# The last path's three products merged into two in the second FFN product: 14 matmuls a tile instead of 15

## The reference, cut to what matters

```python
x = x + xattn(layernorm(x), ctx, mask, Wq, bq, Wk, bk, Wv, bv, Wo, bo)
h = layernorm(x)
x_mixed = k0 * h[s-1] + k1 * h[s] + k2 * h[s+1]
hp = einsum('bsd,pdm->bspm', x_mixed, W1) + b1           # P = 9 paths, m = 64
stacked_paths = einsum('bspm,pmd->bspd', hp, W2) + b2    # d = 256
scores = tanh(x_mixed @ Wo1 + bo1) @ Wo2 + bo2
weights = one_hot(argmax(scores), 9)
collapsed = einsum('bspd,bsp->bsd', stacked_paths, weights)
x = x + layernorm(h + collapsed) * gamma + beta
```

## Time and profile before

| what | value |
|---|---|
| median of 3 runs | 330.58 us (330.08 to 331.59) |
| the profiled execution, its own time | 329.75 us |
| its span, first to last instruction | 328.0 us |
| PE, PEld busy | 303.1 us (92%), 228.2 us (70%) |
| DVE, ACT, POOL busy | 264.7, 181.9, 218.0 us |
| mean granted TensorE clock | 0.994 |

### The profile page before, as it was taken

One profiled execution on the slowest core, in us unless ns is written; L12 is line 12 of the kernel. 1 busy time (PEld: TensorE's weight loads), 2 busy tenths in 40 slices (PEclk: granted clock), 3 DMA queues, 4 the chain that ended last, 5 costly groups with the idle time before them and its releaser, 6 DMA issues. The chain is left out here.

```text
span 328.0 us, 7236 instructions
## 1 busy us (share of the span) xinstructions
PE 303.1 (92%) x2799; PEld 228.2 (70%) x2803; DVE 264.7 (81%) x612; ACT 181.9 (55%) x282; POOL 218.0 (66%) x259
## 2 busy tenths in 40 slices
PE   3889998899989999999999999999999999999991
PEld 2564564566669766896779767886779667967990
DVE  2876799998499796999699796989498878695876
ACT  1455724725963677358853778267552855266520
POOL 0391145872495499957986499957886598539454
PEclk9999999999999999999999999999999999999997
DMA  7942020020020010300120010000100010001003
GB/s 212 242 106 81 2 82 1 2 81 2 1 74 9 0 44 21 82 1 3 66 81 1 2 64 4 2 0 2 66 0 3 1 66 2 0 2 64 3 0 128
DMA packets 20587, 13.16 MB, mean 40 GB/s; under 512 B 10113, under 2 KB 20426, under 8 KB 20554
## 3 DMA queue, kind: packets, MB, share of 16 engines
q1 hardware_dynamic: 18914, 12.14, 12.8%
q10 hardware_dynamic: 1640, 0.57, 0.8%
HBM read 8.51 MB, written 4.19 MB: 39 GB/s over the span
## 5 line engine op out<-in xcount | busy, mean ns | idle before, releaser
L1536 POOL TENSOR_TENSOR rs<-ve,halfneg 128x4 f32<-128x4 f32 x22 | 23.7, 1075 | 37.0 <-DVE ve L1180 37.0
L1630 POOL TENSOR_TENSOR hml<-hs,hmh 128x512 fp32r<-128x512 f32 x28 | 35.1, 1282 | 4.3 <-ACT hmh L985 4.3
L1217 DVE TENSOR_REDUCE mx<-ps 128x16 f32<-128x1024 f32 x32 | 37.6, 1216 | 0.3 <-PE ps L553 0.3
L922 ACT ACTIVATE e<-ps 128x1024 f32<-128x1024 f32 x32 | 31.1, 1023 | 9.5 <-PE ps L592 9.2
L719 PE MATMUL ps<-w2h,hmh 128*128 128x256 f32 (+1 forms) x140 | 35.1, 288 | 0.0
L720 PE MATMUL ps<-w2l,hmh 128*128 128x256 f32 (+1 forms) x140 | 34.1, 280 | 0.0
L1337 DVE TENSOR_TENSOR hs<-hs,ps 128x512 f32<-128x512 f32 x28 | 18.5, 683 | 17.3 <-PE ps L699 17.3
L630 PE MATMUL ps<-wo,osb 128*128 128x256 f32 x128 | 31.4, 390 | 0.2 <-DVE osb L1244 0.2
L1595 POOL TENSOR_TENSOR y<-xh2f,gms 128x256 f32<-128x256 f32 x24 | 20.4, 880 | 16.2 <-DVE xh2f L1189 16.2
L1561 POOL TENSOR_TENSOR x<-xin,bos 128x256 f32<-128x256 f32 x32 | 22.8, 744 | 10.2 <-DVE rDs L1235 9.6
L975 ACT ACTIVATE hs<-ps,b1s 128x512 f32<-128x512 f32 x28 | 19.0, 687 | 16.1 <-PE ps L456 16.1
(11 more groups left out here) (176 smaller groups left out, 804.5 us busy)
## 6 DMA issues: line engine op xcount, KB each, us to landing
xin<-in_x SPq DMA_DIRECT2D x8, 512.0 KB, 3.7
out<-y SPq DMA_DIRECT2D x6, 512.0 KB, 2.9
min_<-in_mask_Bx1xSxS_ik SPq DMA_DIRECT2D x8, 128.0 KB, 3.7
hs<-in_L_ffn_W SPq DMA_DIRECT2D x2, 288.0 KB
hs<-in_L_ffn_W SPq DMA_DIRECT2D x1, 512.0 KB
out<-y SPq DMA_DIRECT2D x2, 256.0 KB, 2.1
out<-xin SPq DMA_DIRECT2D x2, 256.0 KB, 2.3
cst<-in_constants SPq DMA_DIRECT2D x1, 384.0 KB, 6.7
```

The source lines that it names most:

```text
L922: nc.scalar.activation(e[:, 4 * half + g:4 * half + g + 3:2, :], ps[:, 2 + 2 * g:4 + 2 * g, :], ACT.Exp).then_inc(s_e, 1)
L1217: v.tensor_reduce(mx[:, k, :].rearrange("p (a h) -> p a h", a=2), ps[:, bank:bank + 2, :].rearrange("p a (h s) -> p a h s", s=SK), AX.X, A ...
L1536: g.tensor_tensor(ln[7][:, :], ln[6][:, :], halfneg[:, :], ALU.pow).then_inc(s_r, 1)
L1630: g.tensor_tensor(L.lo(m, r), L.selected(m, r), L.hi(m, r).bitcast(F32), ALU.subtract).then_inc(L.s_hl, 1)
```

## The change

Block 4 had 55 unused rows. The change puts path 8's rounded rows a second time into rows 64 to 127 of the remainder's buffer, and W2[8] a second time into rows 64 to 127 of w2h. The matmul lo x w2h of block 4 then gives lo x w2h and hi x w2h of path 8 at once, and the matmul hi x w2h of block 4 is left out. b2 can then no longer come from w2h; its rounded part and its remainder lie instead in rows 64 to 72 and 73 to 81 of w2l, and the one-hot is written twice (columns 0 to 8 and 9 to 17 of the 64 that `rep` passes), so that hi x w2l adds both.

```diff
         def rows_of(m):
-            return P if m < 4 else DM + NPATH
+            return P if m < 4 else DM + 2 * NPATH
+        def lo_rows_of(m):
+            return P if m < 4 else DM
...
+            def hi_below(self):
+                return hml[DM:, NM - 1, :]
...
+            def hi_below(self):
+                return xTl[DM:, 0, :]
...
                 load(w2_32[0:DM, 4, :], W2[8], s_wf)
-                load(w2_32[DM:DM + NPATH, 4, :], b2, s_wf)
+                load(w2_32[DM:, 4, :], W2[8], s_wf)
+                for i in range(2):
+                    load(y[DM + i * NPATH:DM + (i + 1) * NPATH, 1, :], b2, s_wf)
...
             def w2_product(b, j, k, terms, L=usual):
-                        nc.tensor.matmul(o, L.hi(m, r)[:, ks], w2h[0:r, m, :], start=(m == 0), stop=False)
+                        if m < 4:
+                            nc.tensor.matmul(o, L.hi(m, r)[:, ks], w2h[:, m, :], start=(m == 0), stop=False)
                         nc.tensor.matmul(o, L.hi(m, r)[:, ks], w2l[0:r, m, :], start=False, stop=False)
...
                             pe.wait_ge(L.s_hl, L.first + L.count(b, j, NM, m + 1))
-                        mm = nc.tensor.matmul(o, L.lo(m, r)[:, ks], w2h[0:r, m, :], start=False, stop=(m == NM - 1))
+                            if m == NM - 1:
+                                pe.wait_ge(L.s_hb, L.count(b, j, 1, 1))
+                        mm = nc.tensor.matmul(o, L.lo(m, P)[:, ks], w2h[:, m, :], start=False, stop=(m == NM - 1))
...
             def selected_hi(b, j, m, L=usual):
                 nc.scalar.activation(L.hi(m, r), L.selected(m, r), ACT.Copy).then_inc(L.s_hh, 1)
+                if m == NM - 1:
+                    nc.scalar.activation(L.hi_below(), L.selected(m, DM), ACT.Copy).then_inc(L.s_hb, 1)
...
             def ffn_weights_lo():
-                v.tensor_tensor(w2l[0:r, 4, :], w2_32[0:r, 4, :], w2h[0:r, 4, :].bitcast(F32),
-                                ALU.subtract).then_inc(s_w2l, 1)
+                v.tensor_tensor(w2l[0:DM, 4, :], w2_32[0:DM, 4, :], w2h[0:DM, 4, :].bitcast(F32), ALU.subtract)
+                b2_parts = w2l[DM:DM + 2 * NPATH, 4, :]
+                v.tensor_copy(b2_parts, b2_32).then_inc(s_b2h, 1)
+                dve.wait_ge(s_b2h, 1)
+                v.scalar_tensor_tensor(out=b2_parts, in0=b2_parts.bitcast(F32), scalar=cst[DM:DM + 2 * NPATH, C_LB:C_LB + 1],
+                                       in1=b2_32, op0=ALU.mult, op1=ALU.add).then_inc(s_w2l, 1)
...
             def argmax(b, j, L=usual):
-                v.tensor_tensor(oh[:, :, 0:NPATH], iota, per_tile(gidx), ALU.is_equal).then_inc(s_oh, 1)
+                twice = [P, NT, 2, NPATH]
+                v.tensor_tensor(oh[:, :, 0:2 * NPATH].rearrange("p k (a n) -> p k a n", a=2),
+                                cst[:, C_IO:C_IO + NPATH].rearrange("p (k a n) -> p k a n", k=1, a=1).broadcast_to(twice),
+                                gidx[:, :].rearrange("p (k a n) -> p k a n", a=1, n=1).broadcast_to(twice),
+                                ALU.is_equal).then_inc(s_oh, 1)
```

More of the change, by code:

```diff
@@ L58 @@
 C_LO = C_IO + NPATH
-C_CST = C_LO + 1
+C_LB = C_LO + 1
+C_CST = C_LB + 1
 C_BC = C_CST
@@ L92, in constants @@
     c[:, C_LO:C_LO + 1] = np.where(r % 32 < 16, 0, -1)
+    c[:, C_LB:C_LB + 1] = np.where(r < DM + NPATH, 0, -1)
     c[:, C_IO:C_IO + NPATH] = np.arange(NPATH) - NPATH
@@ L190, in layer_program @@
         bc32 = y[:, 0, :].rearrange("p (c n) -> p c n", c=KD)
+        b2_32 = y[DM:DM + 2 * NPATH, 1, :]
         ps = stack.enter_context(nc.psum_tensor("ps", [P, 8, CH], F32))
@@ L247, in layer_program @@
         s_lf, s_lfa, s_lfv = sem("last_ffn_filled"), sem("last_ffn_read_by_act"), sem("last_ffn_read_by_dve")
+        s_hb, s_lhb, s_b2h = sem("last_path_hi_below_lo"), sem("last_chunk_last_path_hi_below_lo"), sem("b2_hi")
         s_lhh, s_lhl, s_lones = sem("last_selected_hi"), sem("last_selected_lo"), sem("last_b2_selector_ones")
@@ L285, in layer_program, with __init__ @@
         class Path:
-            def __init__(self, filled, read_by_act, read_by_dve, hi_done, lo_done):
+            def __init__(self, filled, read_by_act, read_by_dve, hi_done, lo_done, hi_below):
                 self.s_f, self.s_fa, self.s_fv, self.s_hh, self.s_hl = filled, read_by_act, read_by_dve, hi_done, lo_done
+                self.s_hb = hi_below
             def filled(self, b, j, use):
@@ L364, in x @@
                 return ps[:, self.banks[("w2a", "w2b", "w2c")[group]], i * D:(i + 1) * D]
-        usual, last = Usual(s_f, s_fa, s_fv, s_hh, s_hl), Last(s_lf, s_lfa, s_lfv, s_lhh, s_lhl)
-        behind = BehindSteps(s_f, s_fa, s_fv, s_hh, s_hl)
+        usual, last = Usual(s_f, s_fa, s_fv, s_hh, s_hl, s_hb), Last(s_lf, s_lfa, s_lfv, s_lhh, s_lhl, s_lhb)
+        behind = BehindSteps(s_f, s_fa, s_fv, s_hh, s_hl, s_hb)
         last_y = xin[:, 1]
         def rows_of(m):
-            return P if m < 4 else DM + NPATH
+            return P if m < 4 else DM + 2 * NPATH
+        def lo_rows_of(m):
+            return P if m < 4 else DM
         block = stack.enter_context(nc.Block())
@@ L700, in rep @@
                         else:
-                            mm = nc.tensor.matmul(o[DM:, ks], oh[:, k, :], ident_b,
-                                                  start=True, stop=True)
+                            mm = nc.tensor.matmul(o[DM:, ks], oh[:, k, :], ident_b, start=True, stop=True)
                 mm.then_inc(L.s_f, 1)
@@ L881, in split_ffn_weights @@
                 nc.scalar.activation(w2h[:, 0:4, :], w2_32[:, 0:4, :], ACT.Copy)
-                r = DM + NPATH
-                nc.scalar.activation(w2h[0:r, 4, :], w2_32[0:r, 4, :], ACT.Copy).then_inc(s_w2h, 1)
+                nc.scalar.activation(w2h[:, 4, :], w2_32[:, 4, :], ACT.Copy).then_inc(s_w2h, 1)
             def mask_copy(b, j, mask_bank):
@@ L1340, in last_selected_lo @@
             def last_selected_lo(b, j, m):
-                r = rows_of(m)
+                r = lo_rows_of(m)
                 dve.wait_ge(s_lhh, m + 1)
@@ L1714 @@
 WK_LOADS = 4
-WF_LOADS = KD + 1 + 4 + 3 + 4
+WF_LOADS = KD + 1 + 6 + 3 + 4
 _PREFIX = ("L0_xattn_", "L0_ffn_")
```

## The result

The changed kernel takes 327.0 us (median of 4 runs, 326.8 to 327.7) against 330.4 us for the kernel before, measured beside it. The ratio is 0.9904, 95% interval 0.9885 to 0.9924. Two later comparisons of the same two kernels gave 0.9917 (0.9895 to 0.9940) and 0.9917 (0.9894 to 0.9940). By these ratios it is faster by 2.7 to 3.2 us, some 1%; the two medians above differ by 3.4 us. The prediction said 327.7 us and 2.9 us.

The account below looks back on a forecast made before the run. PE was taken to bound the steps (busy 35.99 of 36.36 us). Steps 2.37, POOL -0.2, last step 0 and tail 0.71 summed to 2.9 us, from 330.58 to 327.7 us, range 326.4 to 329.5.

Parts of the forecast that it names:

- The price of a matmul: Second product on PE: each removed matmul is worth its spacing, 0.118 us, so four tiles give 0.47 us a chunk.
- the five steps: Steps one to five: PE bounds them, each shortens by 0.47 us, 2.37 us in all before the loss to POOL.
- rival D: Steps paced by another chain, the matmuls' time becomes waiting; only the tail gains, 0.7 us, 329.9 us; chance 8%.
- POOL's edge: Second product in steps: PE may wait for POOL's remainder of block 4, 0.1 us in two of five steps, -0.2.
- rival B: POOL's remainder takes over in the steps, PE losing 2 x 0.47 us; gain 2.1 us, 328.4 us; chance 15%.
- The last step: Last step: no gain; three tiles' 0.35 us become PE's wait for ACT, the fourth's 0.12 us go the same way.
- rival A: Whole kernel: everything taken off PE shows, 3.8 us, 326.8 us; chance 12%.
- The tail: Tail: six tiles ahead of f1's first residual gain 0.71 us; DVE sets the end, the last two tiles' 0.24 are lost.
- The additions: ACT's copy, doubled one-hot, DVE's start instructions and loads: costed at nothing; ACT's copy in the tail at most 0.1 us.
- rival E: Start: added loads land late and hold up ACT's split, then PE; slower, 333.2 us if they end at 36; chance 4%.
- The sum: Whole kernel: 2.37 - 0.2 + 0 + 0.71 = 2.9 us gained, median from 330.58 to 327.7 us.

Follow-up runs that it names:

- x_putback: Changed kernel with hi x w2h of the last block put back on PE, all additions kept: 330.49 us, ratio 1.0014 to the kernel before.
- x_minus: Changed kernel with hi x w2l of the last block left out as well, 13 matmuls a tile: 325.39 us, ratio 0.9855 to the kernel before.
- the copy moved: Changed kernel with ACT's copy for f0 in the tail placed behind f1's hidden values of blocks 2 and 3: 327.52, 326.50 and 326.98 us.
- the one-hot's experiment: Kernel before with the one-hot of a path written twice (72 elements a partition for 36), nothing else changed: 330.18 us, ratio 1.000.

## Why the prediction was right

**The price of a matmul and the five steps: right.** The spacing stayed at 0.118 us and four of the steps lost 0.46 to 0.51 us each for 0.47 predicted. (The first of the five lost 0.53.) Five of them gave 2.46 us in the profile for 2.37. x_putback shows that the matmuls alone did it, and so rejects rival D.
By the formula of the Trainium skill ("TensorE: Matmul & The Clock Gate", section Back-to-back issue gap), 109 ns, a step would have lost 0.44 us; the measured 0.46 to 0.51 go with the row's 118 ns. That page gives the formula for an isolated single matmul and says that it misses the spacing of a stream in which each matmul has its weight load, as here, so the prediction weighed a figure that was not meant for this case.

**POOL's edge: the place was right, the size was not.** I took 0.1 us in every other step, 0.2 in all. In the five steps it was 0; only in the last step, for which I had not looked at it, did PE wait, 0.11 us that cost nothing. In the step shown the fifth load comes 0.05 us behind POOL's end, as worked out, and the signal fits into that. x_minus shows how near rival B was: one matmul fewer ahead of that point, twice, and nearly half of what is taken out (0.22 of 0.48 us) becomes waiting.

**The last step: right.** PE waits there for POOL (0.11 us) and for ACT (0.22 us), together 0.33 us for the 0.35 that I had given to ACT alone, and then for DVE's last column (0.24 us, for which I had said only that the fourth tile's time goes there). Nothing gained, which rejects rival A. The time alone would not: 327.0 us lies nearer to A's 326.8 than to my 327.7, just outside my own range of 327.1 to 328.3. It is the profile that speaks against A, and with it the two later ratios of 0.9917, whose intervals leave out the 326.8 / 330.58 = 0.9886 that A would give.

**The tail: right in sum, and that is luck.** Predicted 0.71 us, and from the one-hot to the last pair the profiled pair did gain 20.65 - 19.94 = 0.71, but by two errors that cancel. Up to the residual it was 0.50 (DVE's wait there went from 1.54 to 1.28 us, for the 1.1 foreseen), since ACT's copy, costed at nothing, at most 0.1, delayed f1's hidden values by 0.27 us. I had said that the second of these waits for PE anyway; it did not, once the copy stood ahead of it. With the copy moved, 13.80 - 13.03 = 0.77 us are gained there, near the six matmuls' 0.71. Behind the residual the profiled pair gained another 0.21 us, another profile of the same kernel lost 0.37, which leaves it 0.10 us for the tail: that part is where DVE meets POOL, and the prediction has no term for it. The statement that DVE has no wait from there to the end missed that its waits for POOL's instruction are shown as length, not as idle time.

**The additions: right.** The one-hot did not double, DVE's wait at the start was 0.76 us where I expected about 0.4 (the rounding of q took 0.76 us for 1.00, and the added part 0.80 for the 1.0 taken), and ACT waited for no load, which rejects rival E. The one addition that cost something is ACT's copy in the tail.

**The sum.** 2.9 us was forecast for the pair of profiled executions, and 2.69 measured. But 0.49 us at the start are chance; without them it would be 3.2 us. The 0.3 us above the forecast are the 0.2 us taken for POOL, which did not come, and 0.09 us more from the steps. That the number came out within 0.2 us is in part luck as well.

What stays open: how much of the moved copy's 0.27 us reaches the kernel's time in the mean of many executions. The ratios to the kernel before were 0.9931, 0.9885 and 0.9908 with it moved and 0.9904, 0.9917 and 0.9917 without, with intervals of about 0.002 to either side.

## What to carry to other kernels

PE filled these steps to 99%, and an instruction taken from it was worth its spacing (0.118 us), not its recorded length (0.283 us). It was worth nothing in the last step, where PE's next input came from another engine only 0.1 us ahead of PE. Before taking out more, look for the producer that is just in time: here a load that came 0.05 us behind POOL's end did not wait, and one that would have come 0.19 us ahead of it did. Work added to an engine with idle time was free where what is queued behind it had room, and cost 0.27 us in the tail, where it had none; look at the prologue's and the tail's queue apart from the steps'.

## What the hardware showed that I had not expected

A small DVE operation can last as long as POOL's current instruction. The one-hot took from 0.23 to 1.37 us, and an operation on two elements from 0.17 to 0.75 us; in each long case read here its end lay 0.02 to 0.1 us behind the end of a POOL instruction. For the one-hot both inputs are in SBUF, which the rule named with the one-hot's experiment covers. The small TENSOR_SCALAR has a single input and showed the same. For a single input that page of the Trainium skill names only operations in a two-port mode of DVE, and no run here shows in which mode it was.

The start of the kernel differs from one execution to the next: x landed at 6.00 to 7.55 us, and PE's granted clock fell below full in one or two early slices in five of the twelve profiles and in none of the others. From the landing of x to the third group of transposes of the maxima it is 63.49 to 63.52 us in the seven with the full clock, and 64.14 to 66.30 us in the five. The longest had a granted clock of 0.68 from 20 to 24 us and of 0.50 (the 1.2 GHz level) from 24 to 28 us. These 0.6 to 2.8 us are as large as the change itself, and nothing here shows why some executions have them. A difference of 1 us in one pair of profiles therefore says nothing until it is split by place.
